# Angles of the first chunk of generated tables made by GpSimd, with the rounding in two operations

## The reference, cut to what matters

```python
x = x + _L0_cond_ref(x, weights, itok_B_0_15)        # per batch: einsum('bct,bcd->bdt', x, W[condition])
x = x + _L1_cond_ref(x, ..., itok_B_78_3631)         # causal convolution with K, kept where t < length
x = x + _L2_cond_ref(x, ..., itok_B_1_7)             # x @ weight.T + bias + scale * low-rank adapter of the batch
x = x + _L3_cond_ref(x, ..., itok_B_8_3872)          # as L1, on the input cut at its length, other parameters
```

```python
dtA = A * dt[:, None]
Ct = Cc * (jnp.exp(dtA) - 1.0) / A
P = dtA[:, :, None] * jnp.arange(length, dtype=jnp.float32)
K = 2.0 * jnp.einsum('hn,hnl->hl', Ct, jnp.exp(P)).real
y = irfft(rfft(u, n=2L) * rfft(K, n=2L))[..., :L] + u * D
```

## Time and profile before

| | before |
|---|---|
| runs | 1570.95, 1575.60, 1580.62 us |
| median | 1575.6 us |
| profiled execution: its time | 1567.82 us |
| its span on the core | 1565.8 us |
| granted TensorE clock, mean | 0.987 |
| TensorE busy | 1491.0 us (95%) |
| VectorE busy | 1243.7 us (79%) |
| ScalarE busy | 745.7 us (48%) |
| GpSimd busy | 631.1 us (40%) |

### The profile page before, as it was taken

The page is one execution under the profiler, slowest core; times in us unless marked ns, Lnnn a source line. Parts: engine busy times, 40 slices in busy tenths (PEclk is TensorE's granted clock), DMA queues, the critical chain, the costliest instruction groups (busy, mean ns, idle before and its releaser), DMA issues.

```text
span 1565.8 us, 36857 instructions
## 1 busy us (share of the span) xinstructions
PE 1491.0 (95%) x14983; PEld 1289.6 (82%) x14983; DVE 1243.7 (79%) x1495; ACT 745.7 (48%) x1089; POOL 631.1 (40%) x455
## 2 busy tenths in 40 slices
PE   7788769799999999999999999999999999999998
PEld 7777667678888888888888888888888888888887
DVE  8888787879696969696969696978788787969653
ACT  4544544344454545454545454545454444545433
POOL 1211040945454545444343535353545454545030
PEclk9999989899999999999999999999999999999999
DMA  8699968648584858384857657574859483858432
GB/s 297 253 374 395 366 223 273 155 91 225 80 231 100 216 100 224 96 209 120 196 136 176 156 150 182 125 199 111 203 110 217 88 233 80 233 89 229 99 135 69
DMA packets 437847, 283.43 MB, mean 181 GB/s; under 512 B 330536, under 2 KB 377136, under 8 KB 437680
## 3 DMA queue, kind: packets, MB, share of 16 engines
q1 hardware_dynamic: 388784, 175.35, 47.2%
q10 hardware_dynamic: 48928, 106.00, 19.2%
HBM read 159.20 MB, written 73.86 MB: 149 GB/s over the span
## 4 chain that ended last, share of the span: by engine, by line
PE 77%; DVE 10%; DMA 5%; issue 4%; ACT 2%; POOL 2%; ACTq 0%; DVEq 0%; SPq 0%; POOLq 0%
PE ps L1039 36%; PE ps L949 8%; PE ps L1138 7%; PE ps L1015 5%; PE ps L1048 5%; DMA arena<-in_x_dram 5%; PE ps L985 4%; PE ps L1151 3%; PE ps L959 3%; PE ps L841 3%; DVE arena L2021 2%; PE ps L775 1%; DVE gbuf L2012 1%; PE ps L1002 1%; ACT arena L1522 1%
## 5 line engine op out<-in xcount | busy, mean ns | idle before, releaser
L1039 PE MATMUL ps<-arena,w2t 128*128 128x256 f16 x4608 | 525.3, 274 | 9.3 <-ACT arena L1498 4.3
L1039 PEld LDWEIGHTS ps<-arena,w2t 128*128 128x128 f16 x4608 | 452.0, 98 | 67.7 <-issue 4.4
L695 POOL TENSOR_TENSOR arena<-arena 128x68 f32<-128x68 f32 x31 | 26.8, 864 | 696.8 <-DVE arena L2081 395.6
L2124 DVE TENSOR_TENSOR arena<-arena 128x512 f16<-128x512 f32 x128 | 113.7, 889 | 113.4 <-ACT arena L1511 113.4
L841 PE MATMUL ps<-arena 128*128 128x128 f32 x1024 | 136.4, 292 | 47.2 <-DMA arena<-in_x_dram 25.8
L841 PEld LDWEIGHTS ps<-arena 128*128 128x128 f32 x1024 | 127.5, 204 | 54.2 <-DMA arena<-in_x_dram 29.5
L1498 ACT ACTIVATE arena<-ps,biasx 128x256 f32<-128x256 f32 x256 | 103.5, 472 | 132.4 <-PE ps L1039 95.6
L1511 ACT ACTIVATE arena<-arena 128x512 f16<-128x512 f32 x128 | 80.6, 630 | 163.7 <-DVE arena L2120 159.2
L1991 DVE SCALAR_TENSOR_TENSOR arena<-gbuf,arena 128x1024 f16<-128x1024 f32 x60 | 155.3, 2607 | 3.8 <-ACT arena L1432 3.8
L1138 PE MATMUL ps<-arena 128*128 128x256 f16 (+1 forms) x1536 | 137.2, 246 | 1.0
L1138 PEld LDWEIGHTS ps<-arena 128*128 128x128 f16 x1536 | 122.2, 98 | 14.5 <-DVE gbuf L2012 4.6
(11 more groups left out here) (274 smaller groups left out, 2811.6 us busy)
## 6 DMA issues: line engine op xcount, KB each, us to landing
w2t<-w_scratch ACTq DMA_DIRECT2D x96, 512.0 KB, 4.3
arena<-in_x_dram SPq DMA_DIRECT2D x64, 512.0 KB, 9.3
out_dram<-arena SPq DMA_DIRECT2D x64, 512.0 KB, 2.8
gbuf<-x_scratch SPq DMA_DIRECT2D x60, 512.0 KB, 5.3
x_scratch<-arena ACTq DMA_DIRECT2D x25, 960.0 KB, 10.5
gbuf<-w_scratch ACTq DMA_DIRECT2D x32, 512.0 KB, 4.0
arena<-krow_scratch SPq DMA_DIRECT2D x31, 512.0 KB, 8.2
x_scratch<-arena SPq DMA_DIRECT2D x7, 960.0 KB, 10.8
```

The source lines that it names most:

```text
L1039: mm = nc.tensor.matmul(ps[:, bank, n * HW:(n + 1) * HW], weight(p, n, part, k), xx[:, :, k], start=(fresh and n == 0 and k == 0 and q == ...
L2124: tt(x3_quarter(x3l, h0, row), x3part[slot].rearrange("p (k h b) -> p k h b", k=2, h=2), x3_quarter(x3h, h0, row), ALU.subtract).then_inc( ...
```

## The change

The angles of chunk 0, the one of block 0, are made by GpSimd in a new function `first_angles`, called in the first `mix_rows` after the identity has been added and before the mixing. It waits for `turned_copied`, makes the same products and raises the same semaphores (`table_step`, `table_angles`). Its `round_off` has four operations instead of three: VectorE's L1800 subtracts the constant and the angle in one instruction, GpSimd subtracts the constant with a tensor-by-scalar operation, signals a new semaphore `angle_whole`, and then subtracts the angle with a tensor-by-tensor one. All in all 20 instructions instead of 16 come to stand on GpSimd: 8 tensor by tensor, 12 tensor by scalar. Every operation that reads its forerunner's output waits for it. VectorE leaves out the three angle functions in block 0 and makes them in the other blocks as before. The order of every other engine is unchanged.

```diff
+        angle_whole = sem("angle_whole")
...
+            def first_angles():
+
+                pts = nc.gpsimd.tensor_scalar
+                right_steps = steps[:, 0:TB].rearrange("p (q r a) -> p q r a", q=1, r=1).to_broadcast([P, HG, HG, TB])
+                left_steps = steps[:, TB:TB + TL].rearrange("p (q r a) -> p q r a", q=1, r=1).to_broadcast([P, HG, HG, TL])
+
+                def param(n, w):
+                    return turned[:, n, 0:CH].rearrange("p (q r o) -> p q r o", q=HG, o=1).to_broadcast([P, HG, HG, w])
+
+                def round_off(tile, angle, quarter, low, high, n):
+                    pts(tile, angle, quarter, ROUND, ALU.add, ALU.add).then_inc(table_step, 1)
+                    pool.wait_ge(table_step, n)
+                    pts(tile, tile, ROUND, None, ALU.subtract).then_inc(angle_whole, 1)
+                    pool.wait_ge(angle_whole, {2: 1, 4: 2, 8: 3, 10: 4}[n])
+                    ptt(tile, tile, angle, ALU.subtract).then_inc(table_step, 1)
+                    pool.wait_ge(table_step, n + 1)
+                    return pts(tile, tile, low, high, ALU.max, ALU.min)
+
+                pool.wait_ge(turned_copied, 1)
+                ptt(four(angle_r), param(1, TB), right_steps, ALU.mult).then_inc(table_step, 1)
+                pool.wait_ge(table_step, 1)
+                round_off(right_slot(0, 0), four(angle_r), 0.25, -0.25, 0.75, 2)
+                round_off(right_slot(0, 1), four(angle_r), 0.0, -0.5, 0.5, 4).then_inc(table_step, 1)
+                pool.wait_ge(table_step, 6)
+                ptt(four(angle_r), param(0, TB), right_steps, ALU.mult).then_inc(table_angles, 1)
+                ptt(four(angle_l), param(1, TL), left_steps, ALU.mult).then_inc(table_step, 1)
+                pool.wait_ge(table_step, 7)
+                round_off(left_slot(0, 0), four(angle_l), quarter_own, half_own[:, 0:1], half_own[:, 1:2], 8)
+                round_off(left_slot(0, 1), four(angle_l), quarter_adv, half_adv[:, 0:1], half_adv[:, 1:2], 10).then_inc(table_step, 1)
+                pool.wait_ge(table_step, 12)
+                ptt(four(angle_l), param(0, TL), left_steps, ALU.mult).then_inc(table_angles, 1)
+
             def mix_rows(q):
...
+                if q == 0:
+                    first_angles()
                 n = LOT_W + 3 * q
...
-                    if step == 1:
+                    if step == 1 and blk:
                         right_angles(blk, k, i)
-                    if step == 2:
+                    if step == 2 and blk:
                         left_angles(blk, k)
-                    if step == 3:
+                    if step == 3 and blk:
                         adv_angles(blk, k)
```

## The result

Twenty runs of each kernel gave a median of 1577.79 us (1572.26 to 1583.16) after the change against 1572.01 us (1567.36 to 1580.62) before. The ratio of after to before is 1.0033, with a 95% interval of 1.0021 to 1.0045: the change costs 3.3 to 7.1 us, at the middle 5.2 us. It is slower, by less than the 1% that was set as a bound. The profiled execution took 1572.95 us, its span 1571.2 us; like the one before (1567.82 us) it lies near the fastest of its twenty, so the two profiles may be compared.

What follows compares the result with a forecast made beforehand. The DMA hole at 42 to 50 us, ended by VectorE's and ScalarE's chain through chunk 0's angles, was taken to set the time to 200 us. Median 1575.6 + 0.5 gave about 1576 us, range 1567 to 1586.

Steps and rivals of the forecast that it cites:

- The likeliest case: Chunk 0's angles on GpSimd: scalar operations of 0.39 to 0.57 us, whole changed by -0.5 to +1.7 us; 54%.
- the slower rival: ScalarE's wait on the left angles: from 0.45 us per scalar operation, each 0.1 us costs 1.2 us; 1579 to 1588 us; 27%.
- the signs that it named itself: Forecast wrong if scalar operations exceed 0.7 us, loads restart before 51 or after 57 us, or shifts at 54 and 240 differ.
- the hole: No DMA traffic in 42 to 50 us, ahead of full DMA engines; its end sets the time of everything up to 200 us.
- What bounds the start, and what goes: VectorE's 16 angle instructions, 8.2 us, leave before the DMA hole's end; the adapter matrix at 40.9 us allows at most 3.0 us.
- Tensor by tensor and the waits on GpSimd: In GpSimd's angles: eight operations of 0.71 or 0.75 us, 16 waits of 0.08 us, 0.2 us for holding beside VectorE's copy.
- The mixing, costed at nothing: GpSimd's first mixing of weight rows slips to about 47 to 49.5 us; first reader at 60.89 us, 11 us of cover.
- Tensor by scalar: GpSimd's 12 scalar operations in the angles: 0.48 us for 256 elements, 0.50 for 272; bounds 0.30 and 1.42 us.
- What waits for it: Behind the left angles: TensorE's tile 16 5.04 us later, VectorE's copy of tile 15 after 4.5 plus 2.22 us, at 53.7 us.
- break-even: End of GpSimd's left angles at 46.3 to 46.6 us, where the change would neither gain nor lose; 47.0 us was forecast.
- The shift carried through unchanged: From 54 us to the end: DMA engines full to 200 us, so the restart's 0.5 us shift carries through unchanged.
- Collision at 204 us: GpSimd's first tables meet VectorE's angles of chunk 7, should stay; missed or doubled, 5 to 9 us either way; 4%.

Runs made afterwards that it cites:

- no_angles: Chunk 0's angles left out altogether, slots zero-filled by GpSimd, chunks 1 to 7 on VectorE; ratio to before 0.9958 (0.9941 to 0.9976).
- right_gpsimd: Changed kernel with only the right half of chunk 0's angles on GpSimd, left half on VectorE; ratio to before 0.9998 (0.9982 to 1.0014).
- no_clamp: Changed kernel without GpSimd's four clamps (max and min of the rounded angles) of chunk 0; ratio to before 0.9994 (0.9975 to 1.0013).
- copy_price: Changed kernel with its 12 scalar operations of chunk 0 on GpSimd replaced by plain copies; ratio to before 0.9986 (0.9970 to 1.0001).
- left_gpsimd: Changed kernel with only the left half of chunk 0's angles on GpSimd, right half on VectorE; ratio to before 0.9991 (0.9971 to 1.0011).
- adv_gpsimd: Against before: GpSimd makes only chunk 0's second left rounding (five instructions), VectorE the other 13; ratio to before 0.9969 (0.9950 to 0.9988).
- before_apart: Kernel before plus one wait: GpSimd starts the first convolution tables only after VectorE's angles of chunk 7; ratio to before 0.9987 (0.9972 to 1.0002).
- adv_apart: Second left rounding on GpSimd plus first convolution tables held behind the angles of chunk 7; ratio to before 0.9980 (0.9963 to 0.9996).
- price: Changed kernel plus 54 GpSimd instructions timing six kinds at 128, 256 and 1024 elements; at 256 to 1024 a copy costs 0.83 ns an element.

## Why the forecast held, and which term was wrong

The forecast was 1576 us, in a range of 1567 to 1586 us, and 94% for within 1%; 1577.8 us lies in it. The likeliest case was not what happened. It was the slower rival, to which 27% were given. By the signs that it named itself its mechanism is off: the scalar operations cost over 0.7 us, the loads restarted at 60.7 us where 57 was the latest, and a shift of 7.0 us at the hole was 5.5 us at 238 us.

That 1577.8 us stands only 1.8 us from 1576 is luck. The forecast added 0.5 us to 1575.6, the median of three runs of the kernel before, which twenty runs put at 1572.0. Against before +0.5 us was forecast and +5.2 measured; with 1572.0 the same sum would have said 1572.5.

- **What bounds the start, and what goes.** Right, but for one bound. The hole and the two chains that end it stand in the trace of after again, 7.3 and 7.0 us later, and no_angles shows that 8 us of VectorE are worth 3.5 us at the hole's end, 5.1 counted from the parameters. The bound was too tight: VectorE was to be at most 3.0 us earlier at the adapter copy, and no_angles had it 4.9 us earlier, since the matrix landed sooner there. In the changed kernel it landed at 41.4 us and VectorE did wait for it.
- **Tensor by tensor and the waits on GpSimd.** Right: the eight came to 5.55 us against 5.84 worked out. For the holding beside VectorE's adapter copy 0.2 us had been put down; the copy took 0.89 us for 0.68 and GpSimd's clamp beside it 1.19 for 1.07. The mixing, costed at nothing, ended at 56.1 us, well ahead of the transposes at 67.9 that read it.
- **Tensor by scalar.** This is the mis-sized term. The 12 operations took 12.90 us where 5.88 had been put down, 7.0 us more. The selection of the earlier trace rows was taken as nearest because it reads one tensor and writes one, and its 0.29 us served as the lower bound. It says nothing on what an arithmetic step costs there. The bounds, 0.30 to 1.42 us, held the value; the middle of 0.39 to 0.57 was worked out from rates of a fill and of a tensor-by-tensor operation, whereas 2.5 to 3.3 ns an element is above both. The neighbour by kind of instruction wasn't in the trace, and the upper bound deserved more weight.
- **What waits for it.** Right: the copy of tile 15 was to start 4.5 + 2.22 = 6.7 us behind the left angles and tile 16 5.04 us; 6.76 and 5.13 (53.54 to 58.67) were measured.
- **Slower rival, its place and its slope.** Right. 0.1 us a scalar operation was 1.2 us; 7.0 us more on twelve gave a copy of tile 15 at 60.30 us instead of the forecast 53.7. At the end of the angles that was measured, 53.54 us, some 7 us behind break-even, this rival's own scale says about 1583 us.
- **The shift carried through unchanged.** Only about: 6.98 us at tile 15 were 5.6 us at tile 109, over the stretch in which the DMA engines are full, and 5.2 us timed. The sum's own rule would have given 7 us. Over the other kernels hole and time go together loosely: no_angles is ahead by 3.5 us at the hole and by 6.6 us timed, right_gpsimd is late by 4.5 us in its profile and no loss is seen in its times. Part of this is the start of the parameters: counted from them, tile 15 stands at +7.0 us against before in after, +2.1 in no_clamp, +3.8 in right_gpsimd, -0.9 in copy_price, -1.6 in left_gpsimd, -1.4 in adv_gpsimd and -5.1 in no_angles.
- **Collision at 204 us.** It was given 4% to change. In the changed kernel it didn't: 20.0 us from tile 109 to 115, 20.1 before. In left_gpsimd, no_clamp, right_gpsimd and copy_price it took 24.5 to 24.9 us. In the first three of these VectorE's first product of chunk 7 starts inside a large GpSimd operation and takes 1.2 to 2.0 us:

```profile
203.47 1.98 DVE L1850 TENSOR_TENSOR gbuf<-gbuf,steps 128x256 f32<-128x256 f32 x1
```

  That is left_gpsimd; GpSimd's large operation had started at 203.24 us, and of the seven operations behind the product five took 1.9 to 2.5 us and one 1.03. In the kernel before the product ran at 205.71 us in 0.41, ahead of GpSimd's 206.39. From the product to the copy of tile 115 it is 14.3 us there and 11.4 before, so 0.9 us of phase go with 2.9 us; the other 1.7 us of the 4.6 lie ahead of the product. In copy_price the extra time lies ahead of it altogether (14.0 us from tile 109 to the product, 8.7 before), and that wasn't traced further.

What stays open: how much of a shift at 54 us reaches the end. One profiled execution of each kernel can't say. before_apart, whose code is that of before up to 200 us, stood 3.6 us later at tile 15 in its profile, with parameters 1.1 us late and a granted clock of 0.77 from 42 to 50 us (1.00 before); so single markers scatter by as much as the effects between kernels do. The profiled executions of right_gpsimd and before_apart are the slowest of their kernels, those of adv_gpsimd and adv_apart the fastest. Whether right_gpsimd loses anything is open.

## What to carry to other kernels

An engine that is busy on the chain isn't worth its busy time: take the work out and see what comes next, as no_angles did, before paying for its move. Price an instruction of another engine by its own kind, arithmetic included; where the trace has none, take the upper bound seriously, or time it on an idle stretch. Where the receiving engine is slower, move only as much as it ends before the one that waits arrives: five instructions on GpSimd gained 1.9 to 7.9 us where all twenty lost 5.2.

## What the runs showed of the hardware beyond that

- GpSimd's tensor-scalar operation costs 2.5 ns a float32 element with one step and 3.3 with two, against 1.67 for tensor by tensor and 0.83 for a copy; a column as scalar adds 0.06 us at 256 elements (all in price).
- After 5.45 us without a matmul, TensorE's tiles 10 and 11 took 3.75 us for the two where 1.95 is usual; the granted clock of that stretch, 42 to 50 us, was 0.58 on the mean, and 0.50, the lower of its two levels (1.2 GHz), from 44 us on, against 1.00 before. It was hidden here, since both tiles were done before the wait for the left angles ended.
